# A four-convolution stack on 8 x 16 x 512 x 512: output stores moved into the third convolution, projection and plane steps reordered

## The chip, the cores and the metric

One core of one Trainium2 chip runs the kernel. The metric is the device time of one execution in microseconds; the time shown is the median of the runs. The engines are TensorE (PE), VectorE (DVE), ScalarE (ACT), GpSimd (POOL) and SyncE (SP); here SyncE does nothing but issue DMAs and wait.

## The reference

The input x has 8 images of 16 channels of 512 x 512, float32. `_gn` normalises groups of two channels. Four residual layers follow:

```python
x = x + _L0_conv_ref(_gn(x), w_real, w_imag, b_real, b_imag)
x = x + _L1_conv_ref(_gn(x))
x = x + _L2_conv_ref(_gn(x), W)
x = x + _L3_conv_ref(_gn(x), weight)
```

Layer 0 takes rfft2, a complex 3 x 3 convolution in the frequency plane with a bias, and irfft2. Layer 1 gates each row by the sign of its dot product with a sum over rows of the other half of the channels. Layers 2 and 3 are plain 3 x 3 convolutions, 16 to 16 channels, padding 1.

## The kernel before

**Tiling.** An image is cut into 64 strips of 8 rows: 128 partitions (8 rows x 16 channels) by 512 columns, 256 KB each. A pair is two strips, so an image has 32 pairs. The whole image stands in the tile `x1`, written by the first layer, gated, and convolved in place twice.

**Stages of an image.** (1) The transforms: `first_layer` on TensorE, 32 pairs. The 3 x 3 convolution over frequencies becomes a pointwise product with cosines and sines, mixes of channels, and a Hilbert transform along the columns. (2) Sums and gates. (3) The second convolution, strips from the last to the first. (4) Sums again. (5) The third convolution, strips from the first to the last, whose results ScalarE (`evict3`, L662) and VectorE (L1086, L1087) put back into `x1`; from there they are stored. (6) Then the next image. TensorE goes from stage 5 straight into stage 1 of the next.

**A step of the transforms on TensorE** (`step`, L1289): `mix` (L1255) 96 matmuls of pair t; `add_u` (L1263); then for each strip e of the pair before, `hilbert` (L1270) and, for each strip of pair t, `turn` (L1279), which transposes what the mix gave; last `project_next` (L1125 in `project`), which adds two strips of the next image into sums of its columns. `turn` of the odd strip waits for ScalarE's copy (`turned_out`, L576 and L577) of the even strip's, since both use one bank of PSUM; `mix` waits for `y_evicted`, ScalarE's `evict` (L584, L586) of both strips of the pair before the last.

**On VectorE,** a step is `copy_v` (L879, after the mix of the pair), `make_planes` for the pair two ahead (L852 to L863) and two dot products (L890). `make_planes` waits for the strip in `raw`, a tile of two buffers, one for even and one for odd strips. It makes the sum of the halves of the columns (`plus`, L852) and the difference (`minus`, L853), scales the weights (L854), and multiplies the halves by cosines and sines (L858, L860). After L853 it signals `x_taken`, which lets SyncE load the strip after next. The planes of the next image's first two pairs are made during the third convolution, at pairs 20 and 22 (`PLANES_AT`).

**On SyncE,** all DMAs stand in one program, in this order for an image i: the third pair's load; then for each pair `feed`, which loads two strips of the next image for the projection (L433), and the strips of the pair three ahead (`load_x`, L397 to L402) with two tables (L407, after the Hilbert product of an earlier pair); then, behind the first 28 of the 32 feeds, two stores of the image before (L426). After all feeds come the loads of the next image's first two pairs, and after them, during the third convolution, stores of strips 0 to 7, one whenever one of the last eight pairs is evicted (L470 to L474). The last image stores all of its 64 strips there. The two lines that matter for the loads:

```python
sp.wait_ge(x_taken, i * STRIPS + s + 1)                               # L395 load_x
sp.wait_ge(c_stored[k], (i + 1) * STORES + s // STORE_SEMS * 16)      # L425 store
```

`x_taken` begins at 2, so strip s waits until strip s - 2 is out of `raw`. There are four semaphores `c_stored`, so a store waits until the fourth store before it has landed.

Of the kernel before, what the change touches and what calls it, by code (L numbers as in the profile page):

```python
# [29 lines left out]
DEFERRED = STRIPS - 2 * UNROLL  # L30
# [176 lines left out]
def program(nc, x, t_eye, t_hil, t_fix, t_trig, t_strip, t_rows, t_gsel, t_gnext, t_proj, t_zsel, t_fold, t_ends, t_partner, t_eye_mix,  # L207
            t_eye_conv, t_small, t_bias, w_mix, w_u, w_bias, w_conv, out):
    with ExitStack() as ctx:
# [161 lines left out]
        def _(sp):  # L371
# [47 lines left out]
            def store(i, s):  # L419

                k = s % STORE_SEMS
                sp.wait_ge(evicted, ev(i, 1 + STRIPS + s + 1))
                sp.sem_inc(s_sp, 1)
                sp.wait_ge(c_stored[k], (i + 1) * STORES + s // STORE_SEMS * 16)
                sp.sem_inc(s_sp, 1)  # L425
                sp.dma_start(out[i].rearrange("c (s r) w -> s r c w", r=ROWS)[s], x1[:, s, 0:N]).then_inc(c_stored[k], 16)  # L426
# [17 lines left out]
            def image(i, more, stores_left):  # L444
# [14 lines left out]
                for pair in range(DEFERRED // 2):  # L459
                    feed(pair, 2 * pair % TABLES)  # L460
                    if stores_left:
                        for e in range(2):
                            store(i - 1, STRIPS - DEFERRED + pair * 2 + e)
                for pair in range(PAIRS - UNROLL, PAIRS):
                    feed(pair, 2 * pair % TABLES)
# [4 lines left out]
                for n in range(PAIRS):  # L470
                    if more and n >= PAIRS - (STRIPS - DEFERRED):
                        sp.wait_ge(evicted, ev(i, 1 + STRIPS + 2 * n + 2))
                        sp.sem_inc(s_sp, 1)
                        store(i, n - (PAIRS - (STRIPS - DEFERRED)))  # L474
                    elif not more:
                        for e in range(2):
                            store(i, 2 * n + e)
# [208 lines left out]
        def _(dve):  # L686
# [157 lines left out]
            def make_planes(i, pair, slot):  # L844

                for e in range(2):
# [5 lines left out]
                    b.did(V.scalar_tensor_tensor(plus, raw[:, e, 0:HALF], v1(MEAN2), raw[:, e, HALF:N], ALU.subtract, ALU.add))  # L852
                    V.tensor_tensor(minus, raw[:, e, 0:HALF], raw[:, e, HALF:N], ALU.subtract).then_inc(x_taken, 1)  # L853
                    b.then(V.scalar_tensor_tensor(fg(wst[:, k]), fg(mix_s[:, 1]), row_trig[:, 0, bass.ds(s, 1)], fg(mix_s[:, 0]), ALU.mult, ALU.add))  # L854
                    dve.wait_ge(x_taken, i * STRIPS + s + 1 + RAW)
                    for a in range(2):
                        for q in range(2):
                            b.did(V.scalar_tensor_tensor(quarter(planes[:, a, k, :], q, 0), split_in(minus)[:, q, :], 1.0, split_in(trig[:, a, 0:HALF])[:, q, :],  # L858
                                                         ALU.mult, ALU.mult, accum_out=gsum[:, 2 * a + q, bass.ds(s, 1)]))
# [608 lines left out]
```

## Time and profile before

| | |
|---|---|
| runs | 4728.8, 4733.0 (median) and 9641.3 us |
| the profiled execution | 4716.25 us, span 4714.5 us |
| busy: TensorE, VectorE, ScalarE | 4226.5 (90%), 3331.8 (71%), 2541.0 us (54%) |
| mean granted clock of TensorE | 0.959 |
| moved by DMA | 323.6 MB read, 134.2 MB written |
| chain that ended last, by engine | TensorE 60%, VectorE 12%, DMA 8%, issue 8%, SyncE's queue 5%, ScalarE 3% |

The run of 9641.3 us is far outside the other two and stands in no comparison. A row of a group of instructions reads: line, engine, operation, output<-input, shapes, count | busy us, mean ns of one | idle time before them and what ended most of it. A row of the timeline reads: start, length in us, engine, line, operation; in brackets the idle time before it and what ended it. SPq is SyncE's queue of DMA issues: a row with "x8" joins eight of them, from the first's start to the last's end. In the table of stages a row has from:to, its length, then busy us and number of instructions of PE, PEld, DVE, ACT and POOL, then the granted clock, the DMA share and GB/s.

### The profile page before, as it was taken

The page shows a single profiled execution, that of the slowest core. Times are in us where ns is not written, and L with a number is a line of the kernel's source. Part 1 is how long each engine was busy: PE and PEld are TensorE (multiplying, and loading weights), DVE is VectorE, ACT ScalarE, POOL GpSimd, SP SyncE. Part 2 cuts the span into 40 slices and gives each one's busy share as a digit, 9 for nine tenths or more (in the row PEclk, how much of TensorE's full clock was granted, in tenths as well). Part 3 has the DMA queues.
Part 4 walks back from the last instruction along what each step waited for, and adds up shares of the span by engine and source line. Part 5 has one row for each costly group of instructions (what it writes and reads, how often), then busy time and mean ns, then how long its engine had stood idle before and what let it go on. Part 6 is the DMA issues. An engine that isn't in the chain of part 4 may idle for free.

```text
span 4714.5 us, 229091 instructions
## 1 busy us (share of the span) xinstructions
PE 4226.5 (90%) x84848; PEld 2660.6 (56%) x84848; DVE 3331.8 (71%) x13348; ACT 2541.0 (54%) x8637; POOL 1.0 (0%) x6
## 2 busy tenths in 40 slices
PE   4898989989899898998989989899898999988799
PEld 1455765556555566555655556555665556655476
DVE  1887658876588665887658876588756887578873
ACT  4675526655267542775437754377533675335552
POOL 0000000000000000000000000000000000000000
PEclk8999999989999899999999999999999998999999
DMA  7442015520156202661026610356003560034304
GB/s 190 128 136 77 4 40 179 186 82 4 43 184 188 73 4 56 185 187 60 3 66 189 187 46 3 87 184 189 28 3 104 181 185 18 3 99 140 96 4 146
DMA packets 290241, 467.98 MB, mean 99 GB/s; under 512 B 25536, under 2 KB 92288, under 8 KB 289408
## 3 DMA queue, kind: packets, MB, share of 16 engines
q1 hardware_dynamic: 289536, 457.92, 32.2%
q8 instruction: 523, 8.57, 0.8%
q14 instruction: 182, 1.49, 0.1%
HBM read 323.60 MB, written 134.22 MB: 97 GB/s over the span
## 4 chain that ended last, share of the span: by engine, by line
PE 60%; DVE 12%; DMA 8%; issue 8%; SPq 5%; ACT 3%; DVEq 1%; ACTq 1%
PE ps L1352 35%; PE ps L1255 9%; DMA raw<-x 8%; PE ps L1270 4%; PE ps L1263 3%; PE ps L1279 3%; PE ps L1125 2%; DVE shared L858 2%; SPq L426 2%; SPq L433 1%; DVE xin L853 1%; DVE shared L854 1%; ACT x L584 1%; SPq L407 1%; DVE shared L860 1%
## 5 line engine op out<-in xcount | busy, mean ns | idle before, releaser
L1352 PE MATMUL ps<-x,conv_s 32*32 32x512 f32 x49104 | 1753.1, 608 | 76.2 <-DVE x L1016 41.0
L1352 PEld LDWEIGHTS ps<-x,conv_s 32*32 32x32 f32 x49104 | 1246.7, 104 | 520.0 <-issue 290.2
L1255 PE MATMUL ps<-shared 32*32 32x512 f32 x16384 | 654.0, 603 | 0.0
L662 ACT ACTIVATE x<-ps,vec 128x256 f32<-128x256 f32 x512 | 214.6, 470 | 738.6 <-PE ps L1352 738.6
L1270 PEld LDWEIGHTS ps<-hil,shared 128*128 128x128 f32 x4096 | 500.3, 193 | 194.1 <-issue 193.3
L584 ACT ACTIVATE x<-ps,vec 128x128 f32 (+1 forms) x1024 | 376.7, 384 | 430.2 <-PE ps L1270 429.1
L858 DVE SCALAR_TENSOR_TENSOR shared<-xin,trig 128x128 f32<-128x128 f32 x2048 | 530.9, 299 | 106.6 <-DVE shared L854 98.8
L1279 PE MATMUL ps<-eye,vsb 128*128 128x128 f32 x2048 | 369.0, 303 | 222.5 <-DVE vsb L879 127.5
L1270 PE MATMUL ps<-hil,shared 128*128 128x128 f32 x4096 | 567.5, 282 | 0.0
L1086 DVE SCALAR_TENSOR_TENSOR x<-ps,x 128x256 f32<-128x256 f32 x512 | 214.9, 420 | 423.2 <-ACT x L662 422.3
L1255 PEld LDWEIGHTS ps<-shared 32*32 32x32 f32 x16384 | 306.9, 103 | 280.7 <-issue 217.1
L1279 PEld LDWEIGHTS ps<-eye,vsb 128*128 128x128 f32 x2048 | 287.9, 208 | 296.1 <-issue 288.5
L860 DVE TENSOR_TENSOR shared<-xin,trig 128x256 f32<-128x256 f32 x1024 | 434.4, 424 | 0.0
L852 DVE SCALAR_TENSOR_TENSOR xin<-raw,vec 128x256 f32<-128x256 f32 x512 | 247.3, 483 | 243.8 <-DMA raw<-x 243.0
L650 ACT ACTIVATE x<-ps,vec 128x256 f32 x512 | 243.8, 476 | 259.7 <-PE ps L1352 259.7
L601 ACT ACTIVATE zz<-x 128x512 f32 (+1 forms) x512 | 326.4, 638 | 46.0 <-ACT zz L601 44.5
L1032 DVE SCALAR_TENSOR_TENSOR work<-x 128x512 f32 (+1 forms) x256 | 177.2, 693 | 216.3 <-ACT x L652 197.1
L1011 DVE TENSOR_SCALAR x<-x,cols,gate_b (+1 forms) x1024 | 319.8, 364 | 13.6 <-issue 5.7
L1255 PE MATMUL ps<-xin,shared 32*32 32x512 f32 x8192 | 300.5, 611 | 22.8 <-ACT x L586 17.0
L502 ACT ACTIVATE zz<-shared 128x512 f32<-128x512 f32 x448 | 282.7, 631 | 69.0 <-ACT zz L601 28.4
L576 ACT ACTIVATE shared<-ps 128x384 f32<-128x384 f32 x512 | 253.1, 494 | 85.0 <-PE ps L1279 83.5
L890 DVE SCALAR_TENSOR_TENSOR work<-x,colv 128x512 f32<-128x512 f32 x448 | 292.0, 693 | 0.0
(202 smaller groups left out, 4641.5 us busy)
## 6 DMA issues: line engine op xcount, KB each, us to landing
out<-x SPq DMA_DIRECT2D x512, 256.0 KB
shared<-x SPq DMA_DIRECT2D x448, 256.0 KB
raw<-x SPq DMA_DIRECT2D x256, 256.0 KB
raw<-x SPq DMA_DIRECT2D x512, 128.0 KB
shared<-t_strip SPq DMA_DIRECT2D x512, 96.0 KB, 4.0
x<-x SPq DMA_DIRECT2D x64, 256.0 KB, 7.9
x<-t_proj SPq DMA_DIRECT2D x1, 2048.0 KB, 13.3
trig<-t_trig SPq DMA_DIRECT2D x1, 512.0 KB, 9.9
```

Source lines behind the costliest of these rows:

```text
L502: nc.scalar.activation(zz[:], xa[:, k, :], ACT.Square, accum_out=cols[:, 6, bass.ds(s, 1)]).then_inc(a_squared, 1)
L576: nc.scalar.activation(xt[:, e, :, 0:P - TM], flipped[:, :, TM:P], ACT.Identity)
L584: nc.scalar.activation(split_in(side_of(s, 0))[:, q, :], quarter(ps[:, bank, :], q, 0), ACT.Identity, bias=v1(MEAN2), accum_out=sums[:, q, ...
L601: nc.scalar.activation(halves(zz[:]), both_of(s + e), ACT.Square, accum_out=cols[:, 1, bass.ds(s + e, 1)]).then_inc(y_squared, 1)
L858: b.did(V.scalar_tensor_tensor(quarter(planes[:, a, k, :], q, 0), split_in(minus)[:, q, :], 1.0, split_in(trig[:, a, 0:HALF])[:, q, :], AL ...
L860: ins = V.tensor_tensor(planes[:, a, k, HALF:N], plus, trig[:, a, 0:HALF], ALU.mult)
L890: V.scalar_tensor_tensor(halves(planes[:, 0, 0, :] if late else (vc, vy)[e]), both_of(s), 0.5, halves(colv), ALU.mult, ALU.mult, accum_out ...
L1011: steps.did(V.tensor_scalar(of, of, gain, gate_b[:, q, bass.ds(s, 1)], ALU.mult, ALU.add))
L1255: mm = pe.matmul(ps[TM * cg:TM * cg + TM, bank, :], wst[TM * rg:TM * rg + TM, k, v, a, :], of[TM * rg:TM * rg + TM, :], start=(a == AXS), ...
L1270: mm = pe.matmul(quarter(ps[:, BY + 2 * odd + e, :], int(q < 2), q % 2), xt[:, e, q, :], hil[:, q, 0:P], start=False, stop=True, skip_grou ...
L1279: mm = pe.transpose(ps[:, BX, q * P:(q + 1) * P], chunk(q)(vsb[:, e, :]), eye[:])
L1352: mm = pe.matmul(halves(ps[TM * cg:TM * cg + TM, banks[k], :]), conv_s[TM * rg:TM * rg + TM, kw, second, :], x1b[TM * rg:TM * rg + TM, of, ...
```

## The change

Three edits.

**Stores.** `DEFERRED` is now 8, not 56. During the third convolution SyncE has stores of strips 0 to 55, each waiting for its own strip's eviction, written as a loop over four strips at a time; strips 56 to 63 are stored behind the next image's first four feeds. The stores still stand behind the loads of the next image's first two pairs. For the last image all 64 are in the loop.

**Projection.** `project_next` stands between the odd strip's Hilbert product and its transposes.

**Differences first.** `make_planes` computes `minus` before `plus`; `x_taken` is signalled after `plus`; the wait for the weights' scaling is put off to where they are used, and the wait for `x_taken` to where `plus` is.

```diff
-DEFERRED = STRIPS - 2 * UNROLL
+DEFERRED = 2 * UNROLL
...
-            def store(i, s):
-
-                k = s % STORE_SEMS
+            def store(i, s, k, turn):
+
                 sp.wait_ge(evicted, ev(i, 1 + STRIPS + s + 1))
                 sp.sem_inc(s_sp, 1)
-                sp.wait_ge(c_stored[k], (i + 1) * STORES + s // STORE_SEMS * 16)
+                sp.wait_ge(c_stored[k], (i + 1) * STORES + turn * 16)
...
-                for pair in range(DEFERRED // 2):
+                for pair in range(PAIRS):
                     feed(pair, 2 * pair % TABLES)
-                    if stores_left:
+                    if stores_left and pair < DEFERRED // 2:
                         for e in range(2):
-                            store(i - 1, STRIPS - DEFERRED + pair * 2 + e)
-                for pair in range(PAIRS - UNROLL, PAIRS):
-                    feed(pair, 2 * pair % TABLES)
+                            s = STRIPS - DEFERRED + pair * 2 + e
+                            store(i - 1, s, s % STORE_SEMS, s // STORE_SEMS)
                 if more:
                     for pair in range(2):
                         load_pair(i + 1, pair, 2 * pair)
 
-                for n in range(PAIRS):
-                    if more and n >= PAIRS - (STRIPS - DEFERRED):
-                        sp.wait_ge(evicted, ev(i, 1 + STRIPS + 2 * n + 2))
-                        sp.sem_inc(s_sp, 1)
-                        store(i, n - (PAIRS - (STRIPS - DEFERRED)))
-                    elif not more:
-                        for e in range(2):
-                            store(i, 2 * n + e)
+                with sp.Fori(0, (STRIPS - (DEFERRED if more else 0)) // STORE_SEMS) as j:
+                    for k in range(STORE_SEMS):
+                        store(i, j * STORE_SEMS + k, k, j)
...
-                    b.did(V.scalar_tensor_tensor(plus, raw[:, e, 0:HALF], v1(MEAN2), raw[:, e, HALF:N], ALU.subtract, ALU.add))
-                    V.tensor_tensor(minus, raw[:, e, 0:HALF], raw[:, e, HALF:N], ALU.subtract).then_inc(x_taken, 1)
-                    b.then(V.scalar_tensor_tensor(fg(wst[:, k]), fg(mix_s[:, 1]), row_trig[:, 0, bass.ds(s, 1)], fg(mix_s[:, 0]), ALU.mult, ALU.add))
-                    dve.wait_ge(x_taken, i * STRIPS + s + 1 + RAW)
+                    b.did(V.tensor_tensor(minus, raw[:, e, 0:HALF], raw[:, e, HALF:N], ALU.subtract))
+                    V.scalar_tensor_tensor(plus, raw[:, e, 0:HALF], v1(MEAN2), raw[:, e, HALF:N], ALU.subtract, ALU.add).then_inc(x_taken, 1)
+                    b.did(V.scalar_tensor_tensor(fg(wst[:, k]), fg(mix_s[:, 1]), row_trig[:, 0, bass.ds(s, 1)], fg(mix_s[:, 0]), ALU.mult, ALU.add))
+                    b.settle(but=1)
...
+                        if a == 0:
+                            dve.wait_ge(x_taken, i * STRIPS + s + 1 + RAW)
                         ins = V.tensor_tensor(planes[:, a, k, HALF:N], plus, trig[:, a, 0:HALF], ALU.mult)
                         if a == 0:
                             b.did(ins)
+                            b.settle(but=3)
...
-                    for e in range(2):
-                        hilbert(t * 2 - 2 + e, e, 1 - odd)
-                        turn(t, e)
+                    hilbert(t * 2 - 2, 0, 1 - odd)
+                    turn(t, 0)
+                    hilbert(t * 2 - 1, 1, 1 - odd)
                     project_next(2 * (1 - odd), table, uses, first)
+                    turn(t, 1)
```

SyncE's program at the end of image 0, from the second pair's load of the next image to the third's, before (`raw<-x` a load of strips, `shared<-t_strip` tables, `out<-x` stores):

```order
L399 DMA raw<-x 128x1x512
L402 DMA raw<-x 64x1x512 x2
L407 DMA shared<-t_strip 128x192 x2
L426 DMA out<-x 8x16x512 x8
L480 UNCONDITIONAL_BRANCH
L480 ISA
L395 ISA
L399 ISA
L399 DMA raw<-x 128x1x512
```

The same place now:

```order
L399 DMA raw<-x 128x1x512
L402 DMA raw<-x 64x1x512 x2
L407 DMA shared<-t_strip 128x192 x2
L468 UNCONDITIONAL_BRANCH
L468 ISA
L423 ISA
L425 ISA
L425 DMA out<-x 8x16x512
L421 REGISTER_ALU
L425 ISA
L425 DMA out<-x 8x16x512
L421 REGISTER_ALU
```

Eight stores between the two loads have become a loop of 14 turns with four stores each, of which the first two stand here; the third pair's load follows it.

TensorE in the loop over steps, from the even strip's Hilbert product to the next mix, before:

```order
L1270 MATMUL ps<-hil,shared 128x128 x4
L1276 REGISTER_ALU
L1277 REGISTER_ALU
L1279 MATMUL ps<-eye,vsb 128x128 x4
L1270 MATMUL ps<-hil,shared 128x128 x4
L1279 MATMUL ps<-eye,vsb 128x128 x4
L1286 ISA
L1125 MATMUL ps<-shared 64x512 x2
```

And now (the file is four lines shorter above this place):

```order
L1266 MATMUL ps<-hil,shared 128x128 x4
L1272 REGISTER_ALU
L1273 REGISTER_ALU
L1275 MATMUL ps<-eye,vsb 128x128 x4
L1266 MATMUL ps<-hil,shared 128x128 x4
L1282 ISA
L1121 MATMUL ps<-shared 64x512 x2
L1275 MATMUL ps<-eye,vsb 128x128 x4
```

The projection's two matmuls have moved in front of the odd strip's transposes.

## Rows read from the trace of the kernel before

**Rows 1.** The page: GB/s in 40 slices; two of VectorE's costly groups.

```profile
GB/s 190 128 136 77 4 40 179 186 82 4 43 184 188 73 4 56 185 187 60 3 66 189 187 46 3 87 184 189 28 3 104 181 185 18 3 99 140 96 4 146
...
L858 DVE SCALAR_TENSOR_TENSOR shared<-xin,trig 128x128 f32<-128x128 f32 x2048 | 530.9, 299 | 106.6 <-DVE shared L854 98.8
...
L852 DVE SCALAR_TENSOR_TENSOR xin<-raw,vec 128x256 f32<-128x256 f32 x512 | 247.3, 483 | 243.8 <-DMA raw<-x 243.0
```

**Rows 2.** Stages of transforms: first image, last image, sum of images two to seven.

```profile
147.40:426.90 279.50, 260.46 (x3870) 145.95 (x3872) 233.24 (x966) 201.75 (x701) 0.00 (x0) 1.00 0.45 132
4192.20:4462.10 269.90, 234.08 (x3740) 143.05 (x3740) 232.15 (x970) 156.22 (x580) 0.00 (x0) 1.00 0.43 129
...
sum 1732.30, PE 1601.47 PEld 894.79 DVE 1402.00 ACT 1220.08 POOL 0.00; mean PE 266.91 PEld 149.13 DVE 233.67 ACT 203.35 POOL 0.00
```

**Rows 3.** Timeline, a pair of the first image: TensorE, VectorE, ScalarE.

```profile
309.94 1.06 PE L1270 MATMUL ps<-hil,shared 128*128 128x128 f32 x8
311.71 0.72 PE L1279 MATMUL ps<-eye,vsb 128*128 128x128 f32 x4 [0.71 <-ACT shared L577]
312.36 1.08 PE L1125 MATMUL ps<-shared 128*64 128x512 f32 x4
313.37 1.14 PE L1255 MATMUL ps<-xin,shared 32*32 32x512 f32 x32
...
307.68 0.69 DVE L879 COPY vsb<-ps 128x512 f32<-128x512 f32 x1 [0.73 <-PE ps L1255]
...
312.11 0.42 ACT L586 ACTIVATE x<-ps 128x256 f32 x1
```

**Rows 4.** Timeline, a pair of the last image: TensorE, then ScalarE.

```profile
4341.25 1.06 PE L1270 MATMUL ps<-hil,shared 128*128 128x128 f32 x8
...
4344.20 1.15 PE L1255 MATMUL ps<-xin,shared 32*32 32x512 f32 x32 [0.55 <-ACT x L586]
...
4343.33 0.42 ACT L586 ACTIVATE x<-ps 128x256 f32 x1
```

**Rows 5.** Waits on SyncE, 1140 to 1310 us: total, times, longest.

```profile
SPq L397 <- DVE xin L853: 240.6, 3, 234.9
```

**Rows 6.** Timeline of SyncE's queue from the second image to the third.

```profile
1233.93 0.62 SPq L399 DMA_DIRECT2D raw<-x  x1
...
1238.54 0.86 SPq L407 DMA_DIRECT2D shared<-t_strip  x2
1252.59 24.18 SPq L426 DMA_DIRECT2D out<-x  x8
1282.31 0.71 SPq L399 DMA_DIRECT2D raw<-x  x1
```

**Rows 7.** Stores: timeline of two, stage of the last convolution, line L426.

```profile
1448.90 1.81 SPq L426 DMA_DIRECT2D out<-x  x2
1451.02 1.58 SPq L433 DMA_DIRECT2D shared<-x  x2
...
4610.00:4700.00 90.00, 87.39 (x2652) 70.61 (x2630) 38.90 (x110) 22.64 (x54) 0.00 (x0) 0.98 0.50 163
...
L426 SPq DMA_DIRECT2D out<-x x512: 603/682/734, 669.8 to 4708.5; - x171
```

**Rows 8.** Timeline from the second image to the third: TensorE, then VectorE.

```profile
1273.57 1.33 PE L1255 MATMUL ps<-xin,shared 32*32 32x512 f32 x32
...
1287.46 3.79 PE L1255 MATMUL ps<-shared 32*32 32x512 f32 x64
...
1295.11 0.75 PE L1279 MATMUL ps<-eye,vsb 128*128 128x128 f32 x4 [1.70 <-DVE vsb L879]
...
1298.43 1.15 PE L1255 MATMUL ps<-xin,shared 32*32 32x512 f32 x32
1299.32 2.52 PE L1255 MATMUL ps<-shared 32*32 32x512 f32 x64
...
1286.78 0.48 DVE L852 SCALAR_TENSOR_TENSOR xin<-raw,vec 128x256 f32<-128x256 f32 x1 [4.21 <-DMA raw<-x]
```

More of the change, by code:

```diff
@@ L417, in _ @@
                 sp.sem_inc(c_stored[k], STORES)
-            def store(i, s):
-                k = s % STORE_SEMS
+            def store(i, s, k, turn):
                 sp.wait_ge(evicted, ev(i, 1 + STRIPS + s + 1))
                 sp.sem_inc(s_sp, 1)
-                sp.wait_ge(c_stored[k], (i + 1) * STORES + s // STORE_SEMS * 16)
+                sp.wait_ge(c_stored[k], (i + 1) * STORES + turn * 16)
                 sp.sem_inc(s_sp, 1)
-                sp.dma_start(out[i].rearrange("c (s r) w -> s r c w", r=ROWS)[s], x1[:, s, 0:N]).then_inc(c_stored[k], 16)
+                sp.dma_start(out[i].rearrange("c (s r) w -> s r c w", r=ROWS)[s], x1[:, bass.ds(s, 1), 0:N]).then_inc(c_stored[k], 16)
             def load_next(image, s, t, k):
```

## The prediction

> **What bounds the kernel now.** I read the page first. TensorE is the busiest engine throughout, and the GB/s line swings between almost nothing and 180 to 190 once per image [rows 1]: the transforms (the first layer) move all the data, the two convolutions almost none. The time is a chain of stages, and TensorE sets most of each; what the change can touch is the transforms, the hand-over into them, and the third convolution.
>
> The table by stage comes next [rows 2]. It cuts each image's transforms from the third mix to the edge terms, 30 pairs of strips. The first image, which has no stores of a predecessor beside it, takes 279.5 us, 9.32 a pair. Images two to seven take 1732.3 / 6 = 288.7 us, 9.62 a pair. The last, which has stores but no next image to project, takes 269.9 us, 9.00 a pair. So the deferred stores cost about 0.30 us a pair. The page shows where: VectorE stood 243 us in all waiting for raw rows by DMA [rows 1].
>
> Then one pair on TensorE. In the first image the engine stands still once a pair, 0.71 us, between the odd strip's Hilbert product and its transposes, for ScalarE's copy; the projection (1.08) follows, then the next mix, 3.43 us after the odd product began (313.37 - 309.94) [rows 3]. In the last image, without a projection, the same stretch is 2.95 us and it ends on a different wait, ScalarE's eviction at L586 [rows 4]. VectorE has 0.73 us to spare a pair before its copy [rows 3].
>
> Last I read SyncE's queue at a hand-over, where the change is largest. SyncE stood 234.9 us in a single wait at L397, for VectorE to take strip 0 of the next image out of `raw` [rows 5]. The second pair's load is ahead of the stores in program order, there are only two raw buffers, and strip 0 is taken only at pair 20 of the third convolution. That is at 1233.93; SyncE has finished the pair's loads and tables at 1239.4. After that it issues eight stores, one as every second pair is evicted, 1252.59 to 1276.77, jumps back and starts the third pair's load at 1282.31 [rows 6].
>
> **The change part by part.** *Stores.* The diff turns the eight stores into 56, at the same place in the queue: behind the L397 wait. So "stored as evicted" holds only for the last few. At 1239.4, 42 strips or more are evicted and not one is stored. The 56 stores then are a backlog, bounded by DMA and SyncE, and all loads of the next image from its third pair on are queued behind them.
>
> What does one store take in a row of many? The trace shows no long burst, so I bound it. From below: two stores and the step to the next item take 1451.02 - 1448.90 = 2.12 us on SyncE, 1.06 each, when nothing waits [rows 7]. From above: the last store is issued at 4708.5 and the span ends at 4714.5; up to 6.0 us for one, and each store waits for the fourth before it, so 6.0 / 4 = 1.50. Between: the last image's third convolution stored at 163 GB/s, 1.61 us each, but at the pace of the evictions (its DMA share was 0.50), so that is no limit [rows 7]. The page's busiest slice of the later transforms has 189 GB/s, which is 1.39 for 256 KB [rows 1]. I take 1.35, nearest to those, since four in flight at somewhat under 6.0 us each give the same.
>
> 56 x 1.35 = 75.6 us from 1239.4: SyncE is through at 1315.0 rather than 1276.8, a delay of 38.2 us. At 1.06 it would be 22.0, at 1.50 46.6. Does it reach the end? Behind the third pair's load stand VectorE's planes (it waited 4.21 us for that DMA even before, beginning at 1286.78), its copy, TensorE's transposes at 1295.11 (a wait of 1.70 for that copy) and the third mix at 1298.43 [rows 8]. Nothing there has slack of more than a few us; the first mix starts at 1273.57, the second is done soon after 1291 [rows 8], and after those TensorE has nothing to do. All 38.2 us end on the path. There are seven hand-overs: +267 us. The stores read x1 while the third convolution reads it; the last image does so already, and I price it at nothing.
>
> While TensorE stands idle its clock falls: at the present hand-over the second mix's 64 matmuls took 3.79 us, the third's 2.52 [rows 8]. A longer stop should bring more such matmuls into the third pair. Bounds: nothing (VectorE is behind then, and hides it) to twice a pair's 3.6 us of mix less itself, 3.6. I take 2: +14.
>
> *Fewer stores in the transforms.* Eight are left, in the first four pairs. Images two to seven should come to the first image's 9.32.
>
> *Projection between odd product and transposes.* The same matmuls, 1.08 us, now cover ScalarE's 0.71 us. But then the next mix meets the wait of the last image: it can't start before 2.95 us after the odd product. In the first image ScalarE's L586 begins 2.17 us after the product against 2.08 there [rows 3, 4], so 3.04. Saved: 3.43 - 3.04 = 0.39 us a pair, not 0.71. A pair becomes 8.93. The projection's result is wanted only at the end of the stage. In the last image there is no projection: 0.
>
> *Differences first.* VectorE stood 98.8 us in all behind L854, 98.8 / 512 = 0.19 a strip [rows 1]. The new order takes most of that away; the waits it adds look back one and three steps, at work long done. VectorE has room in each pair, so I count 0; without that room it would be 0.39 a pair. `raw` is freed at the same time as before, after both reads.
>
> The shorter pair needs its raw rows sooner. In the first image VectorE's idle time is for TensorE, not for them [rows 3], and the 0.39 us come out of that slack, so I count no new wait.
>
> Sum of the gains: images two to seven, (9.62 - 8.93) x 28 pairs + 0.39 x 2 pairs = 20.1 us each, 121 in all; the first image 0.39 x 30 = 12. Together -133.
>
> **Sum:** +267 + 14 - 133 = +148. The profiled execution took 4716.25 us, so 4864. The other runs lie 12 to 17 us above that (4728.8 and 4733.0, the latter the median shown). I add 16: **4880 us**, 3.1% over the median.
>
> **The rivals.** *The backlog drains fast enough.* If a store costs SyncE's time alone, and less of it than 1.06 (the DMA instruction itself has 0.60 to 0.68 [rows 7]), say 0.82, then 56 take 45.9 us and the delay is 8.5 at each hand-over: +60 and no clock loss, -133: -73, 4643, with the offset 4660, not slower. It decides from (133 / 7 + 37.4) / 56 = 1.01 us a store downwards. For it: DMA share was only 0.50 at 163 GB/s [rows 7]. Against it: the only pairs with their waits met show 1.06. The Trainium skill's page "DMA: Bandwidth & Descriptors" (section Bandwidth) lists 341 GB/s for a load of 1 MB, which by itself would put a 256 KB store at 0.77 us and so speak for this rival; no row here shows that rate.
>
> *The stage keeps its pace.* With the stores gone the pair falls to 9.32 but no further, since the loads of `raw`, still behind the tables' wait for the Hilbert product, come too late for a shorter pair. Gain 0.30 x 28 x 6 = 50 rather than 133: 4963. For it: VectorE's 243 us of waiting [rows 1]. Against it: the last image's pair, at 9.00 with stores beside it, ends on ScalarE and not on those rows [rows 2, 4].
>
> *It does what it says.* Stores leave as evicted, SyncE is free earlier than now, and only the gains are left: 4716 - 133 = 4583, with the offset 4599, faster. Against it: the order of SyncE's queue and the 234.9 us wait. Only if `raw` were taken earlier could this be.
>
> **How the numbers follow.** Forecast as worked out 0.70, fast drain 0.10, pace kept 0.15, as it says 0.05. The range: the forecast with 1.06 a store gives +154 - 133, with 1.50 and a pair's clock loss +326 + 25 - 133; most of its chance lies inside 4790 to 4980, and the upper rival is in there. A change is told from none beyond 2% (4638 to 4828 here). Slower: the forecast but for its low end (a store under 1.22), plus the pace rival, 0.74. Same: that low end and the fast drain, 0.21. Faster: 0.05.
>
> **What would show it.** In the new profile: SyncE's stores begin near 1239 after the same long wait and run without a gap until 1300 or later; the third mix comes 60 us or more after the first, not 25; VectorE's idle time at the plane of the third pair is charged to DMA and is about 40 us, seven times; the transforms' steady pair is 8.9 us, ended by L586; no 0.7 us gap before the odd transposes. I am wrong if the stores begin well before pair 20 of the third convolution, if they pass at 1.0 us each, or if the steady pair stays above 9.2.

## The result, and the profile after

| | before | after |
|---|---|---|
| median of the runs on one chip | 4731.5 us | 4934.8 us (4930.7 to 4940.7, 4 runs) |
| ratio, 95% interval | | 1.0425 [1.0407, 1.0443] |
| profiled execution, its span | 4714.5 us | 4938.9 us |
| mean granted clock of TensorE | 0.959 | 0.929 |

The runs of the kernel before are 4728.8, 4729.9, 4733.0 and the outlier of 9641.3 us; the ratio leaves the outlier out. The changed kernel is 4.25% slower. The forecast was 4880, the range 4790 to 4980. The file is a few lines shorter, so lines differ: the mix is L1251, the Hilbert product L1266, the transposes L1275, the projection L1121, the difference and the sum of the halves L845 and L846, VectorE's copy L875, the stores L425, with their waits at L422 (evicted) and L424 (landed).

The page of the changed kernel first: GB/s in 40 slices, then three costly groups.

```profile
GB/s 184 138 140 47 3 143 154 138 30 3 150 151 140 25 3 156 150 138 22 4 163 151 138 13 4 169 149 134 14 6 169 149 132 14 21 163 82 57 3 139
...
L1275 PE MATMUL ps<-eye,vsb 128*128 128x128 f32 x2048 | 364.6, 302 | 391.1 <-DVE vsb L875 364.6
...
L851 DVE SCALAR_TENSOR_TENSOR shared<-xin,trig 128x128 f32<-128x128 f32 x2048 | 526.1, 297 | 0.0
...
L845 DVE TENSOR_TENSOR xin<-raw 128x256 f32<-128x256 f32 x512 | 214.8, 420 | 404.6 <-DMA raw<-x 402.6
```

Against [rows 1], the transforms' plateau of 180 to 190 GB/s has come down to some 140 (132 to 151): the stores have left it. The 106.6 us that VectorE stood behind the weights at every strip are nought. But VectorE now stands 402.6 us for raw rows instead of 243.0, and one item now leads TensorE's idle time: 364.6 us in front of the transposes, for VectorE's copy.

The stages say where. The same cut as [rows 2], from the third mix to the edge terms: first image, last image, sum of images two to seven (from:to, length, busy us of PE, PEld, DVE, ACT, POOL, clock, DMA share, GB/s).

```profile
146.80:415.90 269.10, 262.42 (x3867) 151.00 (x3870) 227.32 (x965) 198.47 (x699) 0.00 (x0) 1.00 0.47 138
4407.40:4676.20 268.80, 232.18 (x3740) 142.41 (x3740) 227.43 (x966) 155.69 (x579) 0.00 (x0) 1.00 0.27 82
...
sum 1641.00, PE 1577.29 PEld 904.45 DVE 1364.81 ACT 1198.22 POOL 0.00; mean PE 262.88 PEld 150.74 DVE 227.47 ACT 199.70 POOL 0.00
```

The first image gained 10.4 us, images two to seven 1732.3 - 1641.0 = 91.3, the last 1.1: 102.8 in all. All stages of an image, from the starts of the mixes, the edge terms and the third convolution's matmuls in the two timelines (mean of images two to seven; the third convolution of the first seven):

| | before | after |
|---|---|---|
| first to third mix, images two to seven | 24.5 | 70.3 |
| the same, last image | 20.2 | 61.7 |
| third mix to edge terms, images two to seven | 288.7 | 273.5 |
| third convolution, first seven | 124.5 | 125.4 |
| third convolution, last | 108.6 | 113.2 |

(70.3 - 24.5) x 6 + 61.7 - 20.2 = 316 us more at the hand-overs, 103 less in the transforms, 0.9 x 7 + 4.6 = 11 more in the third convolutions: +224, which is what lies between the spans (4938.9 - 4714.5 = 224.4). The 4.6 of the last image are scatter, as is said further down.

The hand-over from the second image to the third, which answers to [rows 6] and [rows 8]. First SyncE's queue, then VectorE, then TensorE.

```profile
1252.42 0.86 SPq L407 DMA_DIRECT2D shared<-t_strip  x2
1254.11 80.31 SPq L425 DMA_DIRECT2D out<-x  x56
1340.26 0.72 SPq L399 DMA_DIRECT2D raw<-x  x1
...
1344.54 0.43 DVE L845 TENSOR_TENSOR xin<-raw 128x256 f32<-128x256 f32 x1 [50.86 <-DMA raw<-x]
...
1286.37 1.41 PE L1251 MATMUL ps<-xin,shared 32*32 32x512 f32 x32
...
1298.58 2.90 PE L1251 MATMUL ps<-shared 32*32 32x512 f32 x64
...
1352.10 1.12 PE L1275 MATMUL ps<-eye,vsb 128*128 128x128 f32 x4 [48.47 <-DVE vsb L875]
1353.02 1.91 PE L1266 MATMUL ps<-hil,shared 128*128 128x128 f32 x8
1354.86 1.98 PE L1121 MATMUL ps<-shared 128*64 128x512 f32 x4
...
1357.72 1.14 PE L1251 MATMUL ps<-xin,shared 32*32 32x512 f32 x32
```

Read it downwards: 56 stores without a gap, 80.31 us; 5.8 us after them, with no other DMA between, the third pair's load (5.5 us before, [rows 6]). VectorE has waited 50.86 us for it, TensorE 48.47 for VectorE, and the third mix comes 71.3 us after the first. The projection takes 1.98 us here against 1.08 in a running image. The granted clock says why; the stop, the rest of the third pair, and what comes behind the third mix:

```profile
1303.60:1352.10 48.50, 0.03 (x2) 0.01 (x1) 6.74 (x30) 1.08 (x5) 0.00 (x0) 0.53 0.49 164
1352.10:1357.70 5.60, 5.60 (x20) 3.55 (x20) 5.52 (x28) 1.74 (x7) 0.00 (x0) 0.51 0.68 187
1357.70:1363.00 5.30, 5.30 (x109) 2.59 (x109) 1.83 (x5) 3.92 (x11) 0.00 (x0) 1.00 0.46 173
```

Over the stop the clock stands at 0.53, and for the 5.6 us after it at 0.51, the lower of TensorE's two levels (1.2 GHz); from the third mix on it is back at 1.00.

Last, a pair of the first image, against [rows 3]; TensorE only.

```profile
303.76 1.06 PE L1266 MATMUL ps<-hil,shared 128*128 128x128 f32 x8
304.75 1.08 PE L1121 MATMUL ps<-shared 128*64 128x512 f32 x4
305.76 0.75 PE L1275 MATMUL ps<-eye,vsb 128*128 128x128 f32 x4
306.81 1.15 PE L1251 MATMUL ps<-xin,shared 32*32 32x512 f32 x32 [0.30 <-issue]
```

The gap of 0.71 us before the odd transposes is gone; the next mix starts 306.81 - 303.76 = 3.05 us after the odd product instead of 3.43. The profile names nothing for its wait of 0.30 us, but the forecast had named ScalarE's eviction (L579 now), and the timeline bears it out:

```profile
305.94 0.43 ACT L579 ACTIVATE x<-ps 128x256 f32 x1
```

The mix comes 0.44 us after the end of this eviction. In [rows 4], where the profile does name the eviction, it comes 0.45 us after; and in all pairs of this stage the distance is 0.44 to 0.54.

### The profile page after: what moved, and what is told of

Read it like the earlier page. It is cut to its first block, busy times and chain, and to the rows that moved or that the text cites. A ratio compares the mean times of both kernels' runs of the same rounds, so it can differ in the third digit from the quotient of the medians.

```text
span 4938.9 us, 230433 instructions
## 1 busy us (share of the span) xinstructions
PE 4220.1 (85%) x84848; PEld 2674.8 (54%) x84848; DVE 3291.7 (67%) x13348; ACT 2518.9 (51%) x8637; POOL 1.0 (0%) x6
## 3 DMA queue, kind: packets, MB, share of 16 engines
q14 instruction: 167, 1.37, 0.1%
## 4 chain that ended last, share of the span: by engine, by line
PE 72%; DMA 8%; issue 6%; DVE 5%; SPq 4%; ACT 2%; ACTq 0%; DVEq 0%
PE ps L1349 30%; PE ps L1251 16%; PE ps L1266 9%; DMA out<-x 6%; PE ps L1275 5%; PE ps L1259 5%; PE ps L1121 4%; SPq L425 3%; DMA raw<-x 2%; ACT x L577 1%; PE ps L1376 1%; DVE shared L851 0%; PE ps L1197 0%; ACT x L579 0%; PE ps L1170 0%
## 5 line engine op out<-in xcount | busy, mean ns | idle before, releaser
L1275 PE MATMUL ps<-eye,vsb 128*128 128x128 f32 x2048 | 364.6, 302 | 391.1 <-DVE vsb L875 364.6
L1251 PE MATMUL ps<-shared 32*32 32x512 f32 x16384 | 665.1, 602 | 0.0
L1266 PEld LDWEIGHTS ps<-hil,shared 128*128 128x128 f32 x4096 | 504.8, 194 | 194.0 <-issue 187.9
L1275 PEld LDWEIGHTS ps<-eye,vsb 128*128 128x128 f32 x2048 | 289.3, 208 | 589.5 <-issue 540.3
L1266 PE MATMUL ps<-hil,shared 128*128 128x128 f32 x4096 | 572.0, 284 | 0.0
L845 DVE TENSOR_TENSOR xin<-raw 128x256 f32<-128x256 f32 x512 | 214.8, 420 | 404.6 <-DMA raw<-x 402.6
L1251 PEld LDWEIGHTS ps<-shared 32*32 32x32 f32 x16384 | 326.7, 104 | 266.8 <-issue 190.7
L875 DVE COPY vsb<-ps 128x512 f32<-128x512 f32 x256 | 176.8, 691 | 304.7 <-PE ps L1251 277.5
L1251 PE MATMUL ps<-xin,shared 32*32 32x512 f32 x8192 | 302.9, 611 | 78.8 <-issue 58.6
```

The source lines that it names most:

```text
L1251: mm = pe.matmul(ps[TM * cg:TM * cg + TM, bank, :], wst[TM * rg:TM * rg + TM, k, v, a, :], of[TM * rg:TM * rg + TM, :], start=(a == AXS), ...
L1266: mm = pe.matmul(quarter(ps[:, BY + 2 * odd + e, :], int(q < 2), q % 2), xt[:, e, q, :], hil[:, q, 0:P], start=False, stop=True, skip_grou ...
L1275: mm = pe.transpose(ps[:, BX, q * P:(q + 1) * P], chunk(q)(vsb[:, e, :]), eye[:])
```

## The experiments

Every ratio is against the kernel before, run on the same chip in the same job (medians 4737.3, 4737.2 and 4733.0 us). Spans and stages are of one profiled execution each. The second convolution, which no edit touches, takes either about 107 or about 111 us an image (the last image 105 or 110), so that its sum over the eight images ranges from 856 to 879 us: spans of single executions carry some 10 us of that. The last section says what the two durations go with. The profiled execution of the kernel before was also one of its fastest (4716 against medians of 4731 to 4737). Where the two disagree, the medians count.

**1. The stores alone.** The changed kernel with the old order of the projection and of the planes:

```diff
-                    hilbert(t * 2 - 2, 0, 1 - odd)
-                    turn(t, 0)
-                    hilbert(t * 2 - 1, 1, 1 - odd)
-                    project_next(2 * (1 - odd), table, uses, first)
-                    turn(t, 1)
+                    for e in range(2):
+                        hilbert(t * 2 - 2 + e, e, 1 - odd)
+                        turn(t, e)
+                    project_next(2 * (1 - odd), table, uses, first)
```

(and `plus` before `minus` in `make_planes`, with its old waits).

> Stores edit alone; projection and plane steps as before. Theory (queue): all 56 stores stand behind SyncE's wait for the raw buffer at pair 20 of the third convolution, and the next image's third-pair load stands behind them. Hand-overs cost 6 x 46 + 41 = +317 us as in the changed kernel; the transforms lose the stores' DMA and their pair falls from 9.62 to 9.3 in images two to seven (-50), the first image stays at 9.32. Expected 4733 + 267 = 5000 us, the steady pair 9.3 and ended by TensorE's gap before the odd transposes. Rival (the other two edits carry nothing, stores do all): the pair falls to 8.97 with the stores edit alone, total 4935.

Measured: 4996.1 us (4987.4 to 4999.6), ratio 1.0548 [1.0509, 1.0587], as the theory had it. The hand-overs are those of the changed kernel, 69.7 us in the mean of images two to seven and 61.8 in the last, and the transforms between them take 281.7 us rather than 288.7. So the loss belongs to the stores; they also bring a gain of 7 us an image, and lose far more.

**2. The other two edits alone.** `DEFERRED` and SyncE's program as before, the projection and the planes as after.

> Projection and plane edits, stores as before. Theory: hand-overs stay near 24 us. The first image's pair becomes 8.97 (-10 us). In images two to seven the loads of raw rows, queued with stores, hold part of it back: the pair falls from 9.62 to about 9.4, -6 each; the last image -1. Expected 4733 - 47 = 4686 us. Rival (the two edits' gain doesn't hang on the stores): 9.62 - 0.35 = 9.27 a pair, -10 in each of seven images, 4662 us.

Measured: 4677.8 us, ratio 0.9873 [0.9832, 0.9913]. Nearer to the theory's figure: behind the loss there is a real gain of these two. But the transforms of images two to seven take 286.0 us, so in them only 2.7 of the 15.2 us come without the stores edit.

**3. What sets the pace of the row of stores.** The loop's stores carry half of their bytes; the other half of those strips' output is not written:

```diff
-            def store(i, s, k, turn):
+            def store(i, s, k, turn, cols_kept=N):
...
-                sp.dma_start(out[i].rearrange("c (s r) w -> s r c w", r=ROWS)[s], x1[:, bass.ds(s, 1), 0:N]).then_inc(c_stored[k], 16)
+                sp.dma_start(out[i].rearrange("c (s r) w -> s r c w", r=ROWS)[s][:, :, 0:cols_kept], x1[:, bass.ds(s, 1), 0:cols_kept]).then_inc(c_stored[k], 16)
...
-                        store(i, j * STORE_SEMS + k, k, j)
+                        store(i, j * STORE_SEMS + k, k, j, HALF)
```

> The changed kernel, but each store of the loop carries only the first half of the columns (128 KB instead of 256 KB); the other half of the output of these strips isn't written. Tells what sets the pace of 1.45 us a store in the row of 56. Theory A (SyncE's instructions set it): pace stays 1.35 to 1.45, time 4935 less at most 40, that is over 4890. Theory B (DMA or the landing of the fourth store before sets it, as the prediction took it): pace falls to 1.1 or less, 7 x 56 x 0.35 = 137 us less, about 4800.

Measured: 4875.4 us, ratio 1.0300 [1.0263, 1.0337], between the two. The trace parts them. SyncE's queue in the run with half the bytes, the first hand-over and the second:

```profile
648.46 64.25 SPq L425 DMA_DIRECT2D out<-x  x56
...
1235.73 76.92 SPq L425 DMA_DIRECT2D out<-x  x56
```

And in the changed kernel: the first hand-over's row, and what SyncE waited for inside the row of the first (us, times, longest) and of the second.

```profile
646.65 77.82 SPq L425 DMA_DIRECT2D out<-x  x56
...
SPq L424 <- DMA out<-x: 14.5, 35, 1.4
...
SPq L424 <- DMA out<-x: 2.8, 9, 0.6
```

At the first hand-over half the bytes shorten the row by 13.6 us, and about that much, 14.5 us, SyncE had waited for the fourth store before to land. At the second they shorten it by 3.4, and the waits were 2.8. The other five rows of 56 are like the second (1.43 to 1.48 us from one store to the next, and 1.37 to 1.39 with half the bytes). So six of seven rows go near the pace of SyncE's own instructions, 1.39 us a store, and one at the pace of the transfers, 1.40, where SyncE without the waits would take about 1.16. The two paces all but coincide in the six rows, so a faster SyncE alone would gain little there. The programs differ: the later images run in a loop, where the image's address is worked out from registers too. SyncE's program from one store to the next, in the first image and in the others:

```order
L425 DMA out<-x 8x16x512
L421 REGISTER_ALU
L425 ISA
L425 DMA out<-x 8x16x512
...
L425 DMA out<-x 8x16x512
L421 ISA
L425 ISA
L425 REGISTER_ALU
L425 DMA out<-x 8x16x512
```

In the changed kernel the register operations of a store (L421 and L425) take 36 and 74 ns in the first image's row. In the second's they take 94 and 138 ns, a third one adds 36, and the DMA instruction itself takes 645 ns instead of 627. Together that is 0.18 of the 0.23 us between 1.16 and 1.39.

The 60 us that the run gained are not all in the rows (13.6 in the first, 23.1 in the six others, 37 in all): the last image's third convolution took 102.6 us instead of 113.2, those of the others 123.6 instead of 125.4. That led to run 8. In the two spans, 11 us more are in the second convolutions, of which fewer took the longer time.

**4. The second pair's load moved between the stores.** SyncE loads the first pair, stores the strips that are evicted by pair 20, loads the second pair when its buffer comes free, and stores the rest:

```diff
                 if more:
-                    for pair in range(2):
-                        load_pair(i + 1, pair, 2 * pair)
-                with sp.Fori(0, (STRIPS - (DEFERRED if more else 0)) // STORE_SEMS) as j:
-                    for k in range(STORE_SEMS):
-                        store(i, j * STORE_SEMS + k, k, j)
+                    load_pair(i + 1, 0, 0)
+                    stores(0, 2 * PLANES_AT[0])
+                    load_pair(i + 1, 1, 2)
+                    stores(2 * PLANES_AT[0], STRIPS - DEFERRED)
+                else:
+                    stores(0, STRIPS)
```

> The changed kernel, but SyncE has the next image's second-pair load between store 39 and store 40, not ahead of store 0, so that the stores leave as evicted. Theory (queue): the hand-over delay of 46 us goes, and SyncE is free about 17 us earlier than in the kernel before, so the hand-over falls to 17 to 22 us (before 24.5): -103 of the transforms and -25 of the hand-overs, 4733 - 128 = 4605 us. Rival (contention: stores beside the third convolution and the hand-over slow TensorE and VectorE wherever they stand): the third convolution grows by 5 us or more an image and the time stays over 4700.

Measured: 4622.6 us (4617.6 to 4628.3), ratio 0.9763 [0.9727, 0.9799], faster than both kernels. SyncE's queue from the second image to the third:

```profile
1204.80 0.66 SPq L399 DMA_DIRECT2D raw<-x  x1
1207.87 1.27 SPq L402 DMA_DIRECT2D raw<-x  x2
1209.25 0.87 SPq L407 DMA_DIRECT2D shared<-t_strip  x2
1210.92 22.39 SPq L425 DMA_DIRECT2D out<-x  x16
1239.54 0.71 SPq L399 DMA_DIRECT2D raw<-x  x1
```

Only 16 stores are left behind the load, 22.39 us, and the third pair's load goes out 3.5 us before the first mix (1243.0) instead of 53.9 after it. The hand-overs take 21.4 us, less than the 24.5 of the kernel before. The position of one load in one queue is worth 312 us (4934.8 - 4622.6). The expectation was 4605; a price came where the rival had looked: the third convolutions of the first seven images take 128.3 us instead of 125.4.

**5. Half the row.** `DEFERRED` 32 instead of 8: 32 stores stand in the row, 32 in the next image's transforms.

> DEFERRED = 32: the row behind SyncE's long wait has 32 stores, not 56, and 32 are left for the first 16 pairs of the transforms. Theory (the cost is the row's length times SyncE's pace, less the 37 us that were there before): 32 x 1.45 = 46.4, so the third pair's load comes 11 us later than in the kernel before and not 45 us, +78 in seven hand-overs; the transforms keep more of their waits for raw rows (279 us from the third mix on, between 273.5 and 286), -67. Expected 4737 + 11 = 4748 us. Rival (cost in proportion to the stores moved): 24 of 48 moved, half of the changed kernel's +203: 4838 us.

Measured: 4741.8 us, ratio 1.0016 [1.0000, 1.0032]. SyncE's row, of which the window shows 31:

```profile
1224.71 44.39 SPq L425 DMA_DIRECT2D out<-x  x31
...
1274.64 0.71 SPq L399 DMA_DIRECT2D raw<-x  x1
```

The hand-overs take 36.4 us. From 32 to 56 stores they grow by 33.9, 1.41 a store; from 8 to 32 by 11.9 only. If the line of the last two points is drawn on, the delay begins at about 32 - 11.9 / 1.41 = 24 stores: a queue with a slack (37.4 us of it, at 1.35 us a store, would have put that point at 28), not a cost in proportion.

**6 and 7. The projection edit alone, the differences edit alone,** on the old stores. Each is its own part of the change's diff on top of the kernel before.

> Projection edit alone. Theory: it carries all of the gain that the two edits had together (-59): the first image's pair falls to 8.97, 4680 us, and the gap before the odd transposes is gone. Rival (VectorE's order matters, since in the hand-over and in pairs late for raw rows VectorE is the one waited for): only two thirds of it, 4698 us.

> Plane edit alone. Theory: VectorE has room in a pair, so its 0.19 us a strip buys nothing in the first image (pair stays 9.32) and little where raw rows are late: 4730 to 4737 us. Rival (VectorE is waited for in late pairs): 64 strips x 0.19 in a part of the pairs, up to 6 us an image, 4700 us.

Measured: projection 4726.5 us, ratio 0.9983 [0.9971, 0.9995]; differences 4685.3 us, ratio 0.9893 [0.9870, 0.9917]. Both the wrong way round from what was expected. In the first image they do just what was argued: its stage is 268.6 us with the projection edit and 279.6 with the differences (279.5 before). With a predecessor's stores beside it, the stage is 292.1 and 285.3 against 288.7. What TensorE and VectorE waited for in the fourth image's stage (third mix to edge terms) shows why. Kernel before, projection edit, differences edit; each first VectorE, then TensorE:

```profile
DVE xin L852 <- DMA raw<-x: 32.9, 24, 2.8
...
PE ps L1279 <- DVE vsb L879: 13.1, 16, 2.0
PE ps L1279 <- ACT shared L577: 7.7, 15, 0.7
```

```profile
DVE xin L852 <- DMA raw<-x: 35.1, 21, 3.5
...
PE ps L1279 <- DVE vsb L879: 17.4, 14, 2.4
PE ps L1255 <- issue: 4.2, 13, 0.4
```

```profile
DVE xin L852 <- DMA raw<-x: 45.7, 28, 4.1
...
PE ps L1282 <- DVE vsb L882: 8.1, 12, 1.6
PE ps L1282 <- ACT shared L577: 10.8, 19, 0.7
```

Before, the transposes wait 16 times in 30 pairs for VectorE's copy, and only 15 times for ScalarE: the stage is held by raw rows that come late, through VectorE. The projection edit removes the 7.7 us for ScalarE and 4.3 more appear behind VectorE, in longer single waits, and 4.2 us of unnamed waits before the mix come on top. The rest is in TensorE's own busy time. The stage before and with the projection edit:

```profile
1879.50:2167.90 288.40, 266.56 (x3868) 148.62 (x3872) 233.63 (x972) 203.24 (x702) 0.00 (x0) 1.00 0.58 180
```

```profile
1862.90:2156.10 293.20, 270.54 (x3864) 152.79 (x3864) 233.07 (x973) 201.79 (x698) 0.00 (x0) 0.98 0.57 177
```

266.56 to 270.54 us at a granted clock of 0.98 instead of 1.00: 4.3 + 4.2 + 4.0 - 7.7 = 4.8, the stage's whole growth (293.2 - 288.4).

The other images show the same. In the transforms of images two to seven the projection edit alone has TensorE at the lower clock (0.50) for 48 us in all; the kernel before has 3 us of that, the differences edit alone 7. For the same matmuls TensorE is busy 1617.6 us instead of 1601.5, 16 of the 20 us by which these six stages grow. So what the projection edit saves in each pair is lost again, for the larger part to the clock. In the fourth image the differences edit frees VectorE of the 12.3 us behind its weights, so it is sooner back after a late row, and 5 us of TensorE's wait for it go.

**8. Half the bytes beside the third convolution,** in the kernel of run 4: the stores of the loops carry columns 0 to 255, the other half of those strips' output is not written.

> As e4_load_between, but each store of the loops carries the first half of the columns (128 KB); the rest of the output of these strips isn't written. Tells what stores beside the third convolution cost. In e4_load_between it took 128.3 us in the mean of images one to seven, in the kernel before 124.5. Theory (the stores' bytes slow the supply of TensorE's instructions): with half the bytes it falls to 124, seven times -4 and -8 in the last image: 4623 - 36 = 4587 us, and TensorE's time under issue falls. Rival (the number of stores, or the waits of VectorE and ScalarE, not bytes): it stays at 128, 4620 us.

Measured: 4566.9 us, ratio 0.9652 [0.9635, 0.9668], 56 us under run 4, 20 more than the theory had. The third convolutions take 123.6 us (128.3) and the last 102.4 (111.0), 41.5 us in all; 14 more between the two spans are in the second convolutions, where no store runs. The last image's convolution, whose stores are at their densest, by what TensorE waited for: in run 4, then with half the bytes. PEld is the weight load, "issue" a wait for nothing that the profile shows.

```profile
PEld ps L1355 <- issue: 18.2, 35, 2.6
PE ps L1355 <- issue: 5.2, 4, 1.7
```

```profile
PEld ps L1355 <- issue: 6.2, 14, 0.7
```

No wait of this stage names a DMA or another engine; what shrinks is the unnamed one, from 23.4 to 6.2 us (the weight loads' part lies partly beside matmuls, so the stage shortens by 8.6 only). The lower clock has the same share of both stages, 5.4 us. So bytes in flight slow TensorE without a semaphore between them. That its supply of instructions suffers, which comes by DMA too (523 packets of queue q8 in the page), would fit, but no run here shows it: in this stage those packets take 1.12 us on average in run 4 and 1.03 with half the bytes. Nor does a run part it from stores and matmuls reading the same tile.

**9 to 11. What each small edit is worth without the row.** The kernel of run 4, with the projection edit undone, with the differences edit undone, and with both undone (the diffs are those of run 1, in part).

> The kernel with the load between the stores, without the projection edit (differences first stays). Theory: the projection edit is worth its 0.35 us a pair wherever no store stands beside the pair, as in the first image (279.5 to 268.6), and it was worth nothing alone only because the stores in the transforms held the pair back. Then its removal costs some 8 to 10 us in each of seven images: steady stage of images two to seven near 282, about 4685 us in all. Rival: differences first carries the gain wherever it is made, stores or none, and the projection is worth nothing beyond the first image: then 4622.6 + 11 = about 4635, steady stage 276 or less.

> The kernel with the load between the stores, without differences first (the projection edit stays). Theory: differences first helps where pairs are late for their raw rows, which is what stores in the transforms brought about; without those stores it is worth little, 0 to 2 us an image: 4622 to 4635 us, steady stage of images two to seven near 275. Rival: it is worth its 50 us (the 7 a hand-over and an image that it gave alone) here too, since its gain is VectorE's own time: about 4670 us, steady stage near 280.

> The kernel with the load between the stores and neither of the two other edits. In the changed kernel the two edits together gave 4996.1 - 4934.8 = 61 us with 56 stores in a row. Theory: the same here, 4622.6 + 61 = about 4684 us, so that the stores edit with its load moved is worth 4737 - 4684 = 53 us by itself. Rival: with no row of stores before them, the two edits are worth as much as they were on the old store order, 59 us, but then projection and differences divide it as they did there (nothing and 50): this run would then equal the one without the projection edit plus nothing, and lie 50 us over the one without differences first's counterpart; the three runs together tell this apart.

Measured: 4665.2, 4658.7 and 4698.5 us. The edits in one table, ratios to the kernel before:

| stores | neither | projection | differences | both |
|---|---|---|---|---|
| as before | 1 | 0.9983 | 0.9893 | 0.9873 |
| 56 in a row | 1.0548 | | | 1.0425 |
| load between | 0.9920 [0.9894, 0.9946] | 0.9824 [0.9779, 0.9868] | 0.9852 [0.9810, 0.9894] | 0.9763 [0.9727, 0.9799] |

The expectations came out half and half. With the stores spread, the projection edit is worth 40 us (4698.5 to 4658.7) and 43 (4665.2 to 4622.6), where it was worth 11 at most on the old stores: the theory holds in direction (its 4685 for run 9 was 20 too much). The differences edit is worth 33 and 36 us here, so the theory that it would fall to nothing is wrong and the rival lay nearer. A stage of images two to seven takes 282.6 us with neither, 281.3 with differences, 278.8 with the projection, 274.7 with both. The two add up: 76 us together, against 40 + 33. Run 11 had been expected at 4684 us, so the two edits are worth 15 more here than in the changed kernel, and the stores edit with its load moved is worth less by itself, 34.5 us (4733.0 to 4698.5) instead of 53. The rest of the differences' gain lies at the hand-over: first to third mix 24.0 without both, 20.9 with differences, 23.5 with the projection.

Part of what the differences edit gives beside the projection edit is the clock again. The kernel without it (run 10) in the fourth image, TensorE at the transposes of one of the first pairs, and the stretch just behind:

```profile
1861.97 0.74 PE L1278 MATMUL ps<-eye,vsb 128*128 128x128 f32 x4 [1.80 <-DVE vsb L878]
...
1863.00:1866.40 3.40, 3.40 (x13) 1.57 (x12) 2.34 (x10) 1.56 (x7) 0.00 (x0) 0.50 0.65 193
```

Five of its images two to seven have two such stretches in their transforms; run 4, which has both edits, has none. TensorE is busy 1595.0 us in these six stages against 1579.5: 15.5 of the 24.4 us between them.

## Why the prediction was right, and where its sizes were off

**The mechanism.** The direction, the place and the chain were right: SyncE's wait at L397 ended late as before, all 56 stores stood behind it, the third pair's load behind them, and the whole delay reached TensorE seven times (51 and 48 us of wait where about 40 was given). Run 1 shows the loss with the stores edit alone, and run 4 takes it away by moving the one load. The rivals fell: "it does what it says" and "drains fast enough" by SyncE's row of 80 us, "keeps its pace" by the pair, at 9.1 us in images two to seven.

**The term of the hand-over, +281 forecast, +316 measured.** Mis-sized by the price of one store. 1.35 us was taken, from four in flight of "somewhat under 6.0 us"; the row measured 80.31 / 56 = 1.43. That is 4.7 us of the difference at this hand-over; the rest is that SyncE's row starts and is left some 2 us later against the first mix (third load 53.9 us after the first mix, 8.7 before: a delay of 45.2, not 38.2). The reasoning behind the price was wrong too: it is landing only in the first image; in the six others it is SyncE's instructions (run 3). The rival that a store costs SyncE's time alone was right in kind there, and wrong in the figure: 1.39, not 0.82. The Trainium skill's page "DMA: Bandwidth & Descriptors" (section Bandwidth) lists 341 GB/s for loads of 1 MB that GpSimd issued. The estimate of 0.77 us for a store of 256 KB that SyncE issues, worked out from it, is not borne out by any row: 256 KB in 1.40 us, where the transfers set the pace, are 187 GB/s.

**The clock, 2 us each.** The size was right: from the first transposes after the stop to the third mix it takes 1357.72 - 1352.10 = 5.6 us, against 1298.43 - 1295.11 = 3.3 before [rows 8]. The forecast looked for it in the third pair's mix; that runs at 1.00, and the slow ones are the transposes, products and projection ahead of it.

**The transforms, -133 forecast, -103 measured.** The sum's pair of 8.93 us is right for undisturbed pairs (269.1 / 30 = 8.97 in the first image), and the 3.04 us between the odd product and the next mix was measured as 3.05, ended by ScalarE's eviction as was said. The step that failed is "images two to seven should come to the first image's": they take 273.5, 4.4 more each, and 4.4 x 6 is 26 of the 30 us missing. About half of the 4.4 is the fifth pair of each of them, 10.4 to 12.0 us against 8.8 in the first image; the first pairs still have eight stores beside them, and raw rows that are late (the one of 12.0 has part of it at the lower clock). The other half is small and in every pair, 0.08 us: there the mix comes 0.54 us after ScalarE's eviction, in the first image 0.44.

**Who earned it.** Here the argument was wrong though the sum was near. The projection was credited with 0.39 us a pair everywhere, the differences with nothing because "VectorE has room in each pair". On the old stores it is the reverse (runs 6 and 7), since the room was read in the first image [rows 3], the one image that has no stores beside it. With a store in the pair, the raw rows are late and VectorE is on the path in half of the pairs. With the stores spread the differences are still worth 33 and 36 us, and there the stages account for it: (282.6 - 281.3 + 24.0 - 20.9) x 6 = 26 and (278.8 - 274.7 + 23.5 - 21.4) x 6 = 37. On the old stores they don't: 288.7 - 285.3 in six images and 1.3 in the last are 22 of the 52 us between the medians, and the spans differ by 24 (4714.5 to 4690.9). The other 28 us are that the profiled execution of the kernel before lies 21 us under its median and that of run 7 lies 7 over its own. Among the 35 executions of the kernel before in these jobs, the four shortest (4719.0 to 4723.0 us) have a mean granted clock of 0.959 to 0.961, the five longest (4747.9 to 4758.0) one of 0.951 to 0.956. Whether the edit keeps such executions from coming is not shown, since no slower one was profiled.

**Stores beside the third convolution, "I price it at nothing".** Wrong, by some 6 us here and more in run 4: 0.9 us an image with the stores at its end, 3.8 with 40 beside it; with half the bytes it is gone. The 4.6 of the last image are not a price of the change: all 64 stores stand beside that convolution in both kernels, and over the eleven kernels that store all bytes it scatters by 5.5 us. In run 2, whose stores are the old ones, it is 3.2 us longer than in the kernel before.

**What was luck.** The terms all missed the same way: 35 at the hand-over, 30 in the transforms and 11 in the third convolutions are the 76 us between +224 and +148. The median was missed by 55 only, because the 16 us added for the slower executions were not needed: the profiled execution of the changed kernel is the longest of its four, 6 us over their median.

## What to carry to other kernels

In a queue that issues in order, look at what stands behind the gated command, not at the command: a load put ahead of its gate holds back everything after it, and what it held back comes out as one row at the end, in front of the next thing that matters. Put the gated load where its gate opens, and fill the time before with what is ready. Price an edit in the image that all the others are like: the first one here had none of the traffic that decided what VectorE's time was worth.

## What the runs showed that was not expected

- SyncE's own time for a store depends on the code around it: 1.16 us each in the first image's code (half the bytes, 56 in a row), 1.39 in the later images', with one register instruction more between two stores and longer ones beside it. That is as long as the transfer of 256 KB takes, 1.40.
- TensorE loses time to another's bytes, without a wait on them: 5 to 9 us of a convolution of 100 to 130 us, in waits that the profile gives no name, gone with half of the bytes (123.6 and 102.4 us against 128.3 and 111.0).
- The second convolution's two durations go with TensorE's clock. It starts at the lower one (0.50) in every image; in all 104 of the thirteen profiles that lasts 2.7 to 4.7 us where the convolution is short (105 to 108 us) and 11.6 to 12.9 us where it is long (110 to 112). In the first two images of the kernel before it is 3.1 and 12.5 us, for 107.1 and 111.8. In the two runs with half the bytes 1 of 16 is long, in the others 35 of 88; why is not known.
